# Three layer norms of a four-layer kernel: logarithm and exponential on ScalarE exchanged for a square root on ScalarE and a reciprocal on VectorE, with four products on TensorE that nobody reads

## The reference

```python
def _ln_t(v, eps=1e-05):
    m = jnp.mean(v, axis=-1, keepdims=True)
    s = jnp.var(v, axis=-1, keepdims=True)
    return (v - m) / jnp.sqrt(s + eps)

t = t + _L2_attn_ref(_ln_t(t), ...)
t = t + _L2_ffn_ref(_ln_t(t), ...)
t = t + _L3_attn_ref(_ln_t(t), ...)
t = t + _L3_ffn_ref(_ln_t(t), ...)
```

## Time and profile before

| | us |
|---|---|
| median of 3 runs | 1770.22 (1770.0 to 1770.23) |
| profiled execution, its own time | 1775.4 |
| its span, first to last instruction | 1773.6 |
| TensorE matmul busy | 1535.2 (87%) |
| VectorE busy | 886.6 (50%) |
| ScalarE busy | 852.8 (48%) |
| GpSimd busy | 317.3 (18%) |
| mean granted TensorE clock | 0.939 of full speed |

### The profile page before, as it was taken

How to read it: one execution, slowest core, us unless ns; L and a number is a source line. 1 busy time by engine, 2 the same in 40 slices (tenths; PEclk the granted TensorE clock), 3 DMA queues, 4 the chain that set the end, 5 groups by cost and what they waited for, 6 DMA issues and landing times. The chain is left out here.

```text
span 1773.6 us, 29966 instructions
## 1 busy us (share of the span) xinstructions
PE 1535.2 (87%) x12396; PEld 772.9 (44%) x12396; DVE 886.6 (50%) x1357; ACT 852.8 (48%) x1161; POOL 317.3 (18%) x135
## 2 busy tenths in 40 slices
PE   6689999999677978999999997999999999448598
PEld 4222222222333755566566565654444444126254
DVE  2468888888733535776777774010001000357242
ACT  3467777777343444677777764122222222231521
POOL 0466666665210001000000000000000000020000
PEclk9589999999898987999999998999999999779889
DMA  1000000000020004343444420000000000000000
GB/s 61 1 2 2 2 2 2 3 2 2 1 77 15 1 1 166 136 156 131 161 167 167 149 102 1 1 0 1 0 1 0 0 0 0 29 0 4 1 0 24
DMA packets 20658, 69.63 MB, mean 39 GB/s; under 512 B 688, under 2 KB 17072, under 8 KB 18096
## 3 DMA queue, kind: packets, MB, share of 16 engines
q1 hardware_dynamic: 20240, 66.73, 10.1%
q10 hardware_dynamic: 288, 1.05, 0.2%
HBM read 33.17 MB, written 34.60 MB: 38 GB/s over the span
## 5 line engine op out<-in xcount | busy, mean ns | idle before, releaser
L489 POOL TENSOR_TENSOR l_work<-l_a_scores,l_work 128x2048 f32<-128x2048 f32 x64 | 233.0, 3642 | 129.7 <-PE banks L607 115.8
L1777 PE MATMUL banks<-s_h,pack_l2f_l3f 128*128 128x512 f32 x512 | 221.0, 592 | 0.0
L1804 ACT ACTIVATE s_h<-banks,pack_l2f_l3f 128x512 f32<-128x512 f32 x128 | 88.0, 688 | 241.8 <-PE banks L1777 175.7
L547 DVE TENSOR_TENSOR l_work<-banks,sc_negc 128x1024 f32<-128x1024 f32 x128 | 156.3, 1221 | 49.7 <-PE banks L654 32.8
L607 PE MATMUL banks<-l_work,pack_l 32*32 32x512 f32 x4096 | 159.8, 607 | 23.4 <-ACT l_work L509 19.7
L509 ACT ACTIVATE l_work<-banks,pack_l 128x1024 f32<-128x1024 f32 x128 | 142.7, 1114 | 76.2 <-PE banks L607 75.4
L1370 PE MATMUL banks<-pack_l2a,r_e 128*128 128x128 f32 x1024 | 142.6, 282 | 26.3 <-ACT r_e L1422 26.3
L1422 ACT ACTIVATE r_e<-banks,r_max 128x1024 f32<-128x1024 f32 x128 | 142.5, 1113 | 44.9 <-DVE r_max L1463 44.8
L1457 DVE TENSOR_REDUCE r_raw<-banks 128x1 f32<-128x640 f32 (+1 forms) x128 | 109.5, 856 | 104.6 <-PE banks L1351 104.6
L1777 PEld LDWEIGHTS banks<-s_h,pack_l2f_l3f 128*128 128x128 f32 x512 | 97.3, 190 | 122.5 <-issue 122.5
L1351 PE MATMUL banks<-r_k,r_q 32*128 32x128 f32 (+3 forms) x832 | 147.9, 464 | 1.1 <-DVE r_v L1295 1.1
(11 more groups left out here) (380 smaller groups left out, 2142.8 us busy)
## 6 DMA issues: line engine op xcount, KB each, us to landing
distances<-r_rd SPq DMA_DIRECT2D x16, 2048.0 KB, 6.3
r_band<-distances SPq DMA_DIRECT2D x16, 1536.0 KB, 7.0
pack_l2f_l3f<-pack_dram_l2f SPq DMA_DIRECT2D x1, 2212.5 KB, 10.2
pack_l2f_l3f<-pack_dram_l3f SPq DMA_DIRECT2D x1, 1248.5 KB, 5.3
pack_l<-pack_dram_l SPq DMA_DIRECT2D x1, 1093.0 KB, 6.4
residual<-x ACTq DMA_DIRECT2D x2, 512.0 KB, 7.6
out<-residual SPq DMA_DIRECT2D x2, 512.0 KB, 3.1
pack_l2a<-pack_dram_l2a SPq DMA_DIRECT2D x1, 715.0 KB, 4.7
```

The costliest lines, as they stand in the source:

```text
L489: pool.tensor_tensor(image(H1R[:, c % 3]), bc(a, 2, 16), bc(b, 3, HW), ALU.add).then_inc(sem("added"), 1)
L547: dve.tensor_tensor(image(H2M[:, (2 * c + part) % 3]), image(PS[:, MAX + j:MAX + j + 2]), bc(NEGC[:, j:j + 2, n, i, rows(half)], 3, HW), A ...
L1777: ins = pe.matmul(bank, W["w2"][:, col:col + P], H1[:, c, m], start=(m == 0), stop=(m == HB - 1))
L1804: act.activation(H[:, c, k], PS[:, g % 8], ACT.Tanh, bias=bias).then_inc(sem("tanh"), 1)
```

## The change

The logarithm and exponential over all four chunks go. In their place ScalarE takes the square root of variance + eps for each chunk, as soon as that chunk's variance is there and between the squares, and VectorE takes the reciprocal of each root, chunk by chunk, ahead of its multiplication. A square root of `eps` into a tile of its own, `table`, stands at the head of ScalarE's stream; nobody reads it. TensorE gets four more products, each after one chunk's reciprocal; they overwrite bank 4, which nobody reads any more. Nothing else in the program is touched.

```diff
@@ -1079,6 +1079,7 @@
         SQ = sb(name + "_sq", [P, 2, CH])
         R = sb(name + "_r", [P, T])
+        table = sb(name + "_table", [P, 1])
         block = ctx.enter_context(nc.Block())
 
         @block.tensor
@@ -1090,29 +1091,32 @@
                     pe.matmul(PS[:, 4 + n], mean, SQ[:, n % 2], start=True, stop=True).then_inc(sem("var"), 1)
+            for n in range(NCH):
+                pe.wait_ge(sem("inverse"), n + 1)
+                pe.matmul(PS[:, 4], mean, X[:, 0:CH], start=True, stop=True)
 
         @block.vector
         def _(dve):
             for n in range(NCH):
                 c = slice(n * CH, (n + 1) * CH)
+                dve.wait_ge(sem("root"), n + 1)
+                dve.reciprocal(R[:, c], R[:, c]).then_inc(sem("inverse"), 1)
                 dve.wait_ge(sem("inverse"), n + 1)
                 dve.tensor_tensor(XN[:, c], PS[:, n], R[:, c], ALU.mult)
 
         @block.scalar
         def _(act):
-            for n in range(NCH):
-                act.wait_ge(sem("centred"), n + 1)
-                if n >= 2:
-                    act.wait_ge(sem("var"), n - 1)
-                act.activation(SQ[:, n % 2], PS[:, n], ACT.Square).then_inc(sem("square"), 1)
-
-            for n in range(NCH):
-                act.wait_ge(sem("var"), n + 1)
-                act.activation(R[:, n * CH:(n + 1) * CH], PS[:, 4 + n], ACT.Ln, bias=eps).then_inc(sem("log"), 1)
-            for n in range(NCH):
-                c = slice(n * CH, (n + 1) * CH)
-                act.wait_ge(sem("log"), n + 1)
-                act.activation(R[:, c], R[:, c], ACT.Exp, scale=-0.5).then_inc(sem("inverse"), 1)
+            act.activation(table[:], eps, ACT.Sqrt)
+            for s in range(NCH + 2):
+                if s < NCH:
+                    act.wait_ge(sem("centred"), s + 1)
+                    if s >= 2:
+                        act.wait_ge(sem("var"), s - 1)
+                    act.activation(SQ[:, s % 2], PS[:, s], ACT.Square).then_inc(sem("square"), 1)
+                if s >= 2:
+                    n = s - 2
+                    act.wait_ge(sem("var"), n + 1)
+                    act.activation(R[:, n * CH:(n + 1) * CH], PS[:, 4 + n], ACT.Sqrt, bias=eps).then_inc(sem("root"), 1)
```

## The result

The changed kernel takes 1802.4 us (median of 4 runs, 1795.5 to 1806.8) against 1770.2 before. The ratio is 1.0178, with a 95% interval from 1.0144 to 1.0213: slower by 1.4 to 2.1%. The forecast was 1796 in a range from 1782 to 1803, so the median lies 0.6 us inside its upper end. The four runs before lie within 0.25 us of one another; 42 later runs of the same kernel spread from 1767.0 to 1775.5, so such closeness was luck. The profiled execution took 1806.8 us, its span is 1805.0 (1773.6 before).

The account below looks back on a forecast made before the run. Each norm was taken as bound by its own serial chain, with VectorE's reciprocal the new bound. Three tails at 8.13 us more (24.4) plus 1.3 for a table load add 25.7 to 1770.2: 1796 us, range 1782 to 1803.

Parts of the forecast that it names:

- What bounds a norm: Three layer norms: each is a separate block costing its own chain; 9.90 us from third square's end to last multiplication.
- The reciprocal: VectorE, each chunk: cost grows by the column, 6.2 ns each, giving 3.33 us at width 512; VectorE becomes the bound.
- The bound of 0.68 below: VectorE reciprocal's lower limit: the pace of the multiplication beside it, 0.68 us at 512 columns.
- rival A: VectorE reciprocal at ordinary pace, about 0.69 us; deciding below some 1.7 us a chunk; result 1750 or 1758; chance 12%.
- the 3.79 above: VectorE reciprocal's upper end that matters: 3.79 us at 512 columns, from the mean of 7.1 ns a column.
- The unread products: TensorE, end of each norm: the fourth ends the block 1.41 us later at low clock, 0.46 at full; low taken.
- Rival B: Reciprocal slow, but unread products hold or regain TensorE's full clock: 11 us less, 1785; chance 10%.
- The early table: Head of ScalarE's stream: load and narrow pass make 1.54 us, some 0.4 late in the third norm, costing nothing.
- The table afterwards: Exponential's table after the norms: load hidden after the first, 1.3 us in the second's successor, nothing new after the third.
- Rival C: ScalarE's square is not in the root's table, so tables reload: 2.6 us a norm, 1804; chance 4%.
- The sum: Whole kernel: 8.13 us more per norm, 24.4 for three, plus 1.3 for the exponential's load, 25.7 us together.
- I take nothing for the next stage: Stages after the norms: no added cost, since they started at the low clock before and will again.

Follow-up runs that it names:

- e3: Changed kernel with a copy of the same 512 columns in place of each VectorE reciprocal, so normed values are wrong: 1756.9 us, ratio 0.9915.
- e5: Changed kernel with ScalarE's single inverse-square-root function replacing the square root and VectorE's reciprocal: 1755.8 us, ratio 0.9906 against the kernel before.
- e6: Changed kernel with each chunk's reciprocal in one, two or eight pieces in the first, second and third norm: 1807.3 us (one run).
- e9: Changed kernel without the early root of eps, so the root's table loads at the first root: 1808.5 us (one run).
- e0: The changed kernel timed again without an edit: 1799.1 us, ratio 1.0164 against the kernel before.
- e4: Kernel before, with the logarithm's table asked for early and logarithms placed between squares by chunk, exponentials kept: 1769.9 us, ratio 0.9988.
- e1: Changed kernel without the four unread products per norm: 1799.6 us, ratio 1.0144 against the kernel before.
- e7: Changed kernel with one more narrow, unread exponential ending ScalarE's stream in each norm, loading the exponential's table there: 1796.3 us (one run).

## Why the prediction was right, point by point

**What bounds a norm.** Right. With the same blocks and barriers, e3 and e5 moved the whole program by what they took out of the tail and what the clock added.

**The reciprocal, 3.33 us from four rows of 1 to 8 columns.** It measured 3.34. The bound of 0.68 below (rival A) and the 3.79 above both fell with that; e6 shows that the line runs through all widths. The condition of rival A was worked out too loosely: 1.7 us a reciprocal makes the tail equal to the old one only without the unread products. With the prediction's own terms, 0.69 + 4 x 0.03 + 3 x 0.60 + 0.69 and 0.46 to 1.41 for the last product, the 9.90 us are reached at 1.3 to 1.5 us. Nothing hangs on it at 3.34. The tail, 0.69 + 15.93 = 16.62 us by the forecast, is 16.63.

**The unread products.** The last ends 1.40 us after the last multiplication, forecast 1.41, at the half clock that was expected: the first product ran at full clock (1.13 us), the other three, 3.98 us apart, at the half one (2.0 to 2.1). Rival B did not come.

**The early table.** Hidden but for some tenths, as said: the first square of the third norm starts 1.37 us after the first product instead of 1.13, 0.24 late where 0.4 was forecast, since the narrow pass takes 0.20 us and not 0.26; the first variance product stands 2.65 us behind the first product in both kernels, so what follows is not later for it. e9 gives the cover's worth.

**The table afterwards.** Right in all three places. Line 1426 has its load beside idle time (1.28 us from 704.34, the exponential right behind it at 705.64); the gates pay 1.28 us. Neither load shows a drain of its own: 0.02 us lie between load and pass. The 2.66 us that the Trainium skill (ScalarE: Activation LUTs, What ACT_TABLE_LOAD costs) gives for a switch is not borne out by any of them. Rival C did not come: no square has a load.

**The sum.** 25.7 us forecast. Measured: 32.2 us by median at first, 27.5 by the medians where e0 ran. By the tails, which do not depend on the head of a norm, it is 3 x 8.1 + 1.3, as forecast. The first profile has 22.4 us in the norms, since the heads of the first two met more full clock than before. Its span grew by 31.4 us: to the 22.4 come 7.6 in the first attention and 2.1 in the gates, the load's 1.3 among them; the other stages together took 0.7 less, though 0.9 of theirs is a term that the prediction did not have, the later landing of the output.

**The step that was too simple** was "I take nothing for the next stage: it started at the low clock before and will again". It did start low, but in the first profile the low clock came back twice in the following 50 us, and the stage took 7.6 us more than before; in e0, the same program, it came back once, and it was 1.5 us. As far as this one profile tells, the 6 us by which the first median lies above the forecast are there and not in the norms. The range held the median by 0.6 us. Its upper end had been put there for a reciprocal of 3.79 us or for 2 to 3 us of the clock's luck, and the reciprocal took none of it: that the range sufficed is partly luck, while the terms of the norms and of the gates' load are not.

## What to carry to other kernels

VectorE's reciprocal costs by the column here, 6.25 ns each from 8 columns to 512, and at 512 it takes some five times as long as a multiplication of the same tile. It belongs on narrow tiles; on a wide one even two passes with two table loads on ScalarE were cheaper (a tail of 9.9 us against 16.6), and one function that gives the inverse root directly was cheapest (4.3). Where only narrow instances of an operation are in a trace, two or three widths give its slope, and the comparison with another operation at the smallest width tells slope from fixed part. Ordering work by chunk and asking for a table early was right: 1.8 to 2.1 us a tail in e4 for both, 1.4 in e9 for the early request. Beside reciprocals that made the tail 6.7 us longer all the same, such a gain does not show in the time.

## What had not been expected of the hardware

- The program of 1.8 ms on one core spreads by 0.2 to 0.6% from run to run. Of twelve profiles of one stage the lengths were 418 to 429 us with 10 to 36 us at a granted clock of 0.50, and its length less half of that time agrees to 2.6 us.
- Reciprocals that follow one another without a wait hide most of their fixed part: 32 of 64 columns took 13.7 us, 4 of 512 columns 13.4.
- The two output transfers at the end landed after 4.0 us instead of 3.1 in the changed kernel and in e0, e1, e3, e7 and e9, and after 3.1 in the others, though their lines are the same in all. From VectorE's last instruction to the span's end it is 6.4 us in the first group and 5.5 in the second. Nothing tried here says why; it is 0.9 us of the difference in span.
